# An attention and mixture-of-experts kernel whose tile loop gets fourfold key weights, summed row statistics and another order of work

## The reference

```python
def block(x, wq, bq, wk, bk, wv, bv, gamma, W1, W2, bias, expert_sel, keys, values):
    q, k, v = (einsum('bchw,oc->bohw', x, w) + b for w, b in ((wq, bq), (wk, bk), (wv, bv)))  # 32, 32, 256 channels
    energy = einsum('bci,bcj->bij', flat(q), flat(k)).reshape(b, h, w, h, w)
    attn = softmax(energy, axis=-1)                 # over rows of 32 keys
    x = gamma * einsum('bchk,bhwkv->bcwv', v, attn) + x
    t = tokens(x)                                   # (b, 1024, 256)
    u = layer_norm(t, eps=1e-5)
    # memory[n, m] = n - m where 0 < n - m <= 32, else 0
    t = t + u @ W1 + (memory @ u) @ W2 + bias
    u = layer_norm(t, eps=1e-5)
    s = sigmoid(u @ expert_sel.T)                   # 32 experts
    val, idx = top_k(s, 2)
    return t + sum over the two experts e of val_e * relu(u @ keys_e) @ values_e
```

## Time and profile before

| | |
|---|---|
| time, median of 3 runs | 505.77 us (504.06 to 508.54) |
| time of the profiled execution | 506.34 us |
| its span, first to last instruction | 504.6 us |
| PE busy | 404.9 us (80%) |
| DVE busy | 376.0 us (75%) |
| POOL busy | 323.5 us (64%) |
| ACT busy | 228.5 us (45%) |

### The profile page before, as it was taken

One profiled execution on the slowest core, in us unless ns is written; L12 is line 12 of the kernel. 1 busy time (PEld: TensorE's weight loads), 2 busy tenths in 40 slices (PEclk: granted clock), 3 DMA queues, 4 the chain that ended last, 5 costly groups with the idle time before them and its releaser, 6 DMA issues.

```text
span 504.6 us, 10093 instructions
## 1 busy us (share of the span) xinstructions
PE 404.9 (80%) x2919; PEld 307.4 (61%) x2919; DVE 376.0 (75%) x1100; ACT 228.5 (45%) x604; POOL 323.5 (64%) x481
## 2 busy tenths in 40 slices
PE   8899999999999999999999865769666597577000
PEld 4667777877778777777676753247454386466000
DVE  2788999999999999999999746648555586657100
ACT  2223554545555455545454434168555396444000
POOL 5355558888778888588888776445555645536610
PEclk9999999999999999999999887699789978878655
DMA  7996001311111111111210011386654343331096
GB/s 221 341 210 159 12 23 54 126 54 45 51 36 43 54 44 54 44 44 44 63 54 35 22 47 59 112 250 186 183 160 145 123 129 107 111 96 51 6 202 125
DMA packets 28439, 49.52 MB, mean 98 GB/s; under 512 B 6204, under 2 KB 21966, under 8 KB 27373
## 3 DMA queue, kind: packets, MB, share of 16 engines
q1 hardware_dynamic: 20512, 26.69, 20.2%
q0 software_dynamic: 7872, 22.19, 14.2%
HBM read 30.74 MB, written 25.73 MB: 112 GB/s over the span
## 4 chain that ended last, share of the span: by engine, by line
PE 48%; DVE 15%; issue 13%; SPq 12%; DMA 2%; POOL 2%; another core or an unknown queue 1%; ACT 1%; DVEq 0%; POOLq 0%; ACTq 0%
PE bank L1217 16%; SPq L412 8%; PE bank L1157 6%; PE bank L1098 5%; PE E L1122 5%; PE bank L1077 2%; PE bank L1190 2%; DVE gmax L765 2%; DVE gsum L813 2%; PE bank L1198 2%; PE bank L1269 2%; PE bank L1177 2%; SPq L274 1%; SPq L409 1%
## 5 line engine op out<-in xcount | busy, mean ns | idle before, releaser
L588 POOL DMA_INDIRECT out<-vT,dest x80 | 79.0, 988 | 63.9 <-DVE vT L1031 43.6
L1217 PE MATMUL bank<-vT,prob 128*128 128x256 f32 x512 | 118.9, 386 | 0.2 <-POOL prob L506 0.2
L1217 PEld LDWEIGHTS bank<-vT,prob 128*128 128x128 f32 x512 | 95.7, 191 | 12.7 <-POOL prob L506 0.6
L506 POOL TENSOR_TENSOR prob<-prob,ginv 128x1024 f32<-128x1024 f32 x32 | 61.1, 1909 | 27.8 <-DVE ginv L828 25.5
L488 POOL DMA_INDIRECT slot_rows<-rows,slot x64 | 68.5, 1070 | 12.6 <-issue 12.6
L685 ACT ACTIVATE prob<-E 128x512 f32<-128x512 f32 x40 | 22.4, 591 | 50.9 <-remote 21.1
L648 ACT ACTIVATE prob<-prob 128x1024 f32<-128x1024 f32 x32 | 33.8, 1056 | 20.6 <-DVE prob L769 20.6
L813 DVE TENSOR_REDUCE gsum<-prob 128x32 f32<-128x1024 f32 x32 | 38.5, 1204 | 4.1 <-ACT prob L648 4.0
L765 DVE TENSOR_REDUCE gmax<-E 128x32 f32<-128x1024 f32 x32 | 39.0, 1219 | 1.8 <-PE E L1122 1.3
L1045 DVE COPY rows<-values_s 64x256 f32 x112 | 37.5, 335 | 3.6 <-issue 2.3
L769 DVE TENSOR_TENSOR prob<-E,gmax 128x1024 f32<-128x1024 f32 x32 | 39.2, 1224 | 1.1
(11 more groups left out here) (211 smaller groups left out, 924.5 us busy)
## 6 DMA issues: line engine op xcount, KB each, us to landing
xc_or_xin<-slot_rows SPq DMA_DIRECT2D x32, 130.0 KB
xt<-x_tok SPq DMA_DIRECT2D x32, 128.0 KB, 2.3
values_s<-values SPq DMA_DIRECT2D x2, 2048.0 KB, 29.1
out<-out POOLq DMA_DIRECT2D x4, 1024.0 KB, 14.5
xc_or_xin<-x_cm SPq DMA_DIRECT2D x3, 1024.0 KB, 22.3
t<-slot_rows SPq DMA_DIRECT2D x16, 130.0 KB
t<-slot_rows SPq DMA_DIRECT2D x32, 65.0 KB
xc_or_xin<-slot_rows SPq DMA_DIRECT2D x32, 65.0 KB
```

The costliest lines, as they stand in the source:

```text
L506: g.tensor_tensor(prob[:, t % 2], prob[:, t % 2], ginv[:, t % 2].unsqueeze(2).to_broadcast([P, WT * KB, W]), ALU.mult).then_inc(prob_done, 1)
L588: g.indirect_dma_start(out=out, out_offset=bass.IndirectOffsetOnAxis(ap=dest[:, n % (2 * NB), k:k + 1], axis=0), in_=yb[:, n % NB, k, :], ...
L1217: mm = m.matmul(av_p, pr[:, j, :], vT[:, b % 2, j, :], start=(j == 0), stop=(j == KB - 1))
```

## The change

- **Fourfold k weights.** The weight tile `wqk` now holds wk four times and wq once. k comes out of TensorE in all four groups of 32 partitions and is evacuated whole; q is projected by 8 matmuls of 128 rows by 32 columns, so that the four 32-token parts of a tile land in four partition groups (`q_s[c*32:(c+1)*32]`). `energies` then uses 16 positions of the array, the row group c writing PSUM bank c of a new 4-bank tile `X`.
- **When.** q is projected in step 2 of a batch, k in quarters in steps 3 to 6. k's evacuation moves from VectorE to ScalarE (except for the first batch). v is evacuated one step later.
- **Accumulated sums.** `bn_stats` and `bn_aggr` go. The residual sums become `scalar_tensor_tensor` with `accum_out` (sum of the row), ScalarE then does `Square` of (sum - 256 x) with `accum_out`, and adds eps in another activation; GpSimd keeps the power and the shift.
- **Order on TensorE.** memory and second transpose lead, then attention, positions, logits, projections, mix, v, transpose. v waits for `t1_done` of the attention in the same step, since `v_p` shares bank 7 with `av_p`.
- **Scatters** of a tile go in one place, one step later, ahead of the second layer norm's factors on GpSimd.
- **Routing tail.** sigmoid, top-2 (`MAX`, `MAX_INDEX`) go to the end of VectorE's step, one-hot and positions' sums into the next step.

The diff, cut to its core:

```diff
-QK_STEPS = (5, 6)
+Q_STEP, K_STEPS = 2, (3, 4, 5, 6)
...
-        E = ps("E", [P, WT * KB * W])
-        bank = {i: ps(f"bank{i}", [P, 512]) for i in range(2, 8)}
+        X = ps("X", [P, 2048])
+        bank = [X[:, i * 512:(i + 1) * 512] for i in range(4)] + [ps(f"bank{i}", [P, 512])[:, :] for i in range(4, 8)]
+        E = X.rearrange("p (w c) -> p w c", w=WT)[:, :, 0:KB * W]
...
+        qk_p = bank[6][:, C:2 * C]
+        av_p = bank[7][:, 0:C]
+        v_p = bank[7][:, C:2 * C]
...
-            def layer_norm_factors(t, mv_t, mv_done, rstd, used, ve_done, rstd_done, nmr_done):
-                pool.wait_ge(mv_done, t + 1)
+            def layer_norm_factors(t, mv_t, rstd, used, ve_done, rstd_done, nmr_done):
+                pool.wait_ge(ve_done, t + 1)
                 after(pool, used, t - 1)
-                g.tensor_scalar(rstd[:, t % 2, 0:1], mv_t[:, 1:2], LN_EPS, None, ALU.add).then_inc(ve_done, 1)
...
-                for t in tiles(s, S_SEND):
-                    rows_complete(t)
-                    scatter_rows(t, 0)
+                for t in tiles(s, S_SEND + 1):
+                    send(t)
                 for t in tiles(s, S_NORM2):
                     second_factors(t)
...
+            def squared(x, mv_t, rstd_t, t, x_done, rstd_done, mv_done, ve_done):
+                act.wait_ge(x_done, t + 1)
+                after(act, ve_done, t)
+                a.activation(squares[:, :], x, ACT.Square, bias=mv_t[:, 0:1], scale=-float(C),
+                             accum_out=mv_t[:, 1:2]).then_inc(mv_done, 1)
+                act.wait_ge(mv_done, t + 1)
+                after(act, rstd_done, t - 1)
+                a.activation(rstd_t[:, 0:1], mv_t[:, 1:2], ACT.Identity, bias=eps_col[:, 0:1], scale=1.0 / C ** 3).then_inc(ve_done, 1)
...
+            def first_sum(t):
+                dve.wait_ge(av_mm, t + 1)
...
+                v.scalar_tensor_tensor(out=t1[:, t % 3], in0=av_p, scalar=1.0, in1=xt[:, t % 4], op0=ALU.mult, op1=ALU.add,
+                                       accum_out=mv1[:, t % 2, 0:1]).then_inc(t1_done, 1)
...
-                v.tensor_tensor(t2[:, t], h_at(t), t1b[:, t % 2], ALU.add).then_inc(t2_done, 1)
-                dve.wait_ge(t2_done, t + 1)
-                v.bn_stats(bn2[:, t % 2], t2[:, t]).then_inc(bn2_done, 1)
...
+            def k_proj(b, u):
+                per = HW // len(K_STEPS)
+                for a in range(CH):
+                    mm = m.matmul(qk_p, wqk[:, a, 0:4 * QK], xc[:, b % 2, a, u * per:(u + 1) * per],
+                                  start=(a == 0), stop=(a == CH - 1))
+                mm.then_inc(k_mm, 1)
+            def q_proj(b, dst):
+                for a in range(CH):
+                    tokens = xc[:, b % 2, a, :].rearrange("p (t w h) -> p w t h", w=WT, h=H)
+                    for c in range(WT):
+                        mm = m.matmul(dst[c * QK:(c + 1) * QK, :], wqk[:, a, 4 * QK:5 * QK], tokens[:, c],
+                                      start=(a == 0), stop=(a == CH - 1))
+                mm.then_inc(q_mm, 1)
...
-                for w in range(WT // 2):
+                for c in range(WT):
                     for g in range(WT):
-                        for r in range(2):
-                            at = slice((2 * r + 1) * QK, (2 * r + 2) * QK)
-                            cols = slice((r * 2 + w) * KB * W, (r * 2 + w + 1) * KB * W)
-                            mm = m.matmul(E[g * H:(g + 1) * H, cols], q_s[at, b % 2, tb, w, :],
-                                          k_s[at, b % 2, g].rearrange("p j v -> p (j v)"), start=True, stop=True)
+                        at = slice(c * QK, (c + 1) * QK)
+                        mm = m.matmul(E[g * H:(g + 1) * H, c, :], q_s[at, b % 2, tb, :],
+                                      k_s[at, b % 2, g].rearrange("p j v -> p (j v)"), start=True, stop=True)
...
+            for s in range(NT):
+                if s > 1:
+                    energies(s)
...
+                for t in tiles(s, S_NORM2):
+                    memory(t)
+                for t in tiles(s, S_ROUTE):
+                    second_turn(t)
+                for t in tiles(s, S_AV):
+                    attend(t)
+                for t in tiles(s, S_POS):
+                    positions(t)
+                for t in tiles(s, S_ROUTE):
+                    logits(t)
...
+                for t in tiles(s, S_MIX):
+                    mix(t)
+                if work:
+                    after(pe, t1_done, s)
...
+                    v_proj(work[0], work[1], v_p)
```

More of the change, by code:

```diff
@@ L641, in _ @@
[L641 to L648 removed]
+                    logits_exp(t)
                 if s == 0:
@@ L669, in _ @@
                 for t in tiles(s, S_ROUTE):
[L670 to L678 removed]
+                    columns_written(t)
@@ L824, in _ @@
-                t = tile(s, 0)
-                if t is not None:
-                    dve.wait_ge(sum_done, t + 1)
-                    after(dve, prob_done, t - 1)
-                    v.reciprocal(ginv[:, t % 2], gsum[:, t % 2]).then_inc(inv_done, 1)
+                for t in tiles(s, S_SEND):
+                    place(t)
+                for t in tiles(s, S_POS):
+                    chosen(t)
+                for t in tiles(s, S_SEND):
+                    entry_rows(t)
+                for t in tiles(s, S_POS):
+                    both_chosen(t)
@@ L1192, in _ @@
-                for t in tiles(s, S_ROUTE):
-                    pe.wait_ge(u2T_out, t + 1)
-                    after(pe, ex_done, t)
-                    if proj_work(s - 1) and proj_work(s - 1)[2]:
-                        pe.wait_ge(v_out, bank6_v[0])
-                    for a in range(CH):
-                        mm = m.matmul(lg_p, u2T[:, t % 2, a, :], sels[:, a, :], start=(a == 0), stop=(a == CH - 1))
-                    mm.then_inc(lg_mm, 1)
-                t = tile(s, S_POS)
-                if t is not None and s < NT + S_MIX:
-                    positions(t)
+                    second_turn(t)
@@ L1219, in _ @@
-                if work:
-                    for c in work[2]:
-                        qk_proj(work[0], c)
-                t = tile(s, S_TURN)
-                if t is not None:
-                    pe.wait_ge(u1_done, t + 1)
-                    after(pe, uT_lo_done, t)
-                    for a in range(CH):
-                        mm = m.transpose(uT_p[:, a, :], u1[:, t % 2, a * P:(a + 1) * P], ident[:, :])
-                    mm.then_inc(uT_mm, 1)
-                if s < NT:
-                    for t in tiles(s, S_MIX):
-                        mix(t)
-                elif s == NT + 1:
+                for t in tiles(s, S_AV):
+                    attend(t)
@@ L1234, in _ @@
+                for t in tiles(s, S_TURN):
+                    turn(t)
+                if s == NT + 1:
                     mix(NT - 1)
-                if work and work[2]:
-                    v_proj(work[0], work[1])
-                    bank6_v[0] = v_evacs[0]
             for _ in range(PLAN_WARM):
-                m.matmul(bank[7][:, :], ones_b[:, :], warm[:, :], start=True, stop=True)
+                m.matmul(bank[7], ones_b[:, :], warm[:, :], start=True, stop=True)
             pe.wait_ge(sched_done, 4)
```

634 lines of the change are left out of this document (326 added, 308 removed).

## The result

The changed kernel takes 517.08 us (median of 4 runs, 514.66 to 523.37), the kernel before 506.98 beside it. 498.5 was forecast, in a range of 493 to 507.

A forecast was written before the change was run, and what follows sets the result against it. TensorE was taken to bound the middle batches, VectorE the last. Terms -4.4 + 0.5 - 4.8 - 0.4 + 1.8 = -7.3 gave 498.5 us against the median of 505.77; range 493 to 507.

The forecast's parts named there:

- the one on the routing chain: VectorE, last batch: four dependent operations no longer interleaved cost 0.3 us more a step (0 to 0.5).
- rival (c): Slower: exponential late behind a ScalarE normalisation that waits for GpSimd, which waits for eps; 513 us, chance 0.1.
- Energies: TensorE, each step: 32 passes on 16 positions instead of 8, 0.64 us for 1.02, 0.38 saved.
- rival (a): Row groups don't overlap four deep, energies stay at 1.02 us; 506.5 us, chance 0.1.
- Two middle batches: TensorE: each full batch from 70.14 to 67.95 us through shorter energies, projections and fewer waits; -4.4 for two.
- The prediction's own ring: Energies, maximum, VectorE up to the residual sum, v, transpose, next energies; TensorE reaches v at 6.93 without a projection.
- Projections: TensorE, each batch: k stays at 3.44 us as four quarters of 0.86; q adds 1.05.
- Sums: VectorE: accumulated sums replace statistics instructions, 0.96 becomes 0.42 and 0.90 becomes 0.45, 0.99 us less a step.
- -5.2 was forecast for that batch: Last batch, VectorE-bound: seven steps of 7.5 for 8.18 us, -4.8, and the first maximum 0.4 sooner, -0.4.
- v's wait: v waits for the residual sum, ending 6.8 us after the energies' start; hidden except in the first steps.
- The head: First batch: v's unhidden wait and early k quarters delay it, steps 5 and 6 give back about 3; net +0.5.
- Drain: Behind the last maximum: longer layer norm chains and later work, against less GpSimd time; +1.8 us (-1 to +5).

The follow-up runs named there:

- a1: Changed kernel with the addition of 1 to the exponentials also writing its row sum to an unread column: 502.95 us, ratio 0.995.
- b2: Kernel of a1 with VectorE's low part of z ahead of v's evacuation: 500.93 us, ratio 0.992.
- a2: Changed kernel with the addition of 1 written as a sum of two SBUF tensors: 522.3 us, ratio 1.036.
- b1: Kernel of a1 with the statistics as before (bn_stats, bn_aggr) in place of accumulated sums and ScalarE's squares: 511.92 us.
- b4: Kernel before with the accumulated sums alone; order, energies, projections and scatters unchanged: 510.81 us, ratio 1.014.
- c1: Changed kernel, addition in its original form, GpSimd's scaling of the weights split into two instructions of half the columns: ratio 1.009.
- a3: Kernel before with one more constant addition on VectorE behind the residual sum, under GpSimd's scaling: 558.3 us, ratio 1.108.
- b3: Kernel of b2 with the one-hot comparison and its sum moved to the end of VectorE's step: 508.49 us.

## Why the prediction was wrong

The stretches of four kernels, from maximum to maximum of the tile named, in us:

| | before | forecast | after | a1 | b2 |
|---|---|---|---|---|---|
| start to tile 8 | 79.0 | 79.5 | 81.35 | 80.5 | 80.0 |
| 8 to 16 | 70.1 | 67.95 | 73.1 | 69.6 | 68.8 |
| 16 to 24 | 70.2 | 67.95 | 73.1 | 69.5 | 68.6 |
| 24 to 31 | 57.0 | 51.8 | 60.65 | 51.0 | 51.0 |
| last maximum to plan | 39.5 | 41.3 | 41.5 | 42.1 | 41.2 |
| plan to end | 188.8 | 188.8 | 191.8 | 188.8 | 188.4 |

**The step that failed** is the one on the routing chain: "no longer interleaved with other work: four dependent operations ..., 0.3 more (0 to 0.5)". I priced the moved operations by their dependences, with durations from rows in which GpSimd was elsewhere, and asked for no operation what its neighbour engine would be doing at the new place. 1.95 for 0.15 is +1.8 us of VectorE a step. It puts VectorE on the chain of six steps of eight in the middle batches and of all in the last: 9.05 for a1's 8.14 without a projection, 9.05 to 9.57 for 8.76 to 9.26 with one, and 8.65 for 7.32 in the last batch. It turned -5.6 at the last maximum (a1) into +12.0 (after): 17.6 us in the trace. By the medians a1 and after are 14 apart, a1 and a2 (held alike, on a1's chip) 19. The range's upper end of 507 contained no such term; rival (c), slower through a late exponential, had the right sign and the wrong mechanism: ScalarE and GpSimd do not stand in after's chain from tile 8 to the last maximum. Without the hold the forecast was still too good by 4 us (a1) and 2 (b2), and the terms below say where: of the -9.1 forecast at the last maximum, a1 has -5.6 and b2 -7.9.

**Energies: right in size.** 0.64 forecast, 0.64 to 0.65 measured (b2's chain), against 1.02 in the earlier trace rows: what two bursts of sixteen positions were to take, so rival (a) is out. Where VectorE waits for their end they take 0.81 for 1.11. The half that the prediction drew from the Trainium skill, TensorEngine Tiling (Array Packing), 0.51, was not reached.

**Two middle batches: -4.4 forecast, -2.9 in b2 and -1.2 in a1.** In b2 0.38 a step is gained with the energies, and memory, now right behind them, takes 0.67 for 0.47, attention 3.46 for 3.55, the second transpose 0.22 for 0.37, mix 1.47 for 1.40, the rest 0.73 for 0.63; a step is 8.04 for 8.30, where 7.93 was forecast. I carried the other pieces over from the old order unchanged. The prediction's own ring held a better number: v comes at 6.93, and with v's 0.86 and the transpose's 0.22 behind it that makes a step of 8.01. Projections: k adds 0.85 (0.86 forecast), q 1.13 (1.05). In a1 v's evacuation ahead of the low part costs another 0.1 a step.

**Sums: right.** The instructions are 0.36 and 0.42 with the read 0.08 beside them; b1 puts their worth at 0.86 us a step in the last batch (0.99 forecast). -5.2 was forecast for that batch, -6.0 came in a1 (7.3 a step for 7.5). There the bound is not VectorE, as forecast, but in most steps a ring that the prediction hadn't: TensorE's memory to mix 6.40, z's high part on ScalarE 0.39, its low part on VectorE 0.44, signals, and memory again, 7.32 us. One step in a1's chain, from the maximum at 248.83, is VectorE alone and takes 7.08. ScalarE's read of the accumulator is 0.19, of which 0.10 stands behind the square's end (0.05 forecast), and no step of b2's chain between tile 8 and the last maximum has a square in it; b4 shows such terms on the chain where the order is the old one.

**v's wait: right.** In a1 the residual sum ends 6.5 after the energies' start (6.8 forecast) and v follows the mix without a gap. Before tile 8 it binds as forecast: in after, v at 27.52 right behind the sum (27.10 + 0.36), the third energies at 28.58 (28.4 forecast, 26.75 before). The head lost 1.0 to 1.5 where 0.5 was forecast, and 2.3 in after, with the held addition.

**Drain: +1.8 forecast, +1.7 to 2.6 measured.** Behind the loop the addition isn't held, 0.17 us.

**What stays open.** By the trace a2 and after differ by 0.1 at the last maximum, and by 2.4 us in span; by medians they are 5 us apart. In after's trace the last maximum comes 12 us later than in before's and the drain is 2 us longer, which with 507 for the kernel before would make 521; the runs other than the profiled one took 514.66 to 517.66. The expert stage's length differs between executions (191.8 us in after's trace, 188.8 in before's) and was 33 us shorter on the third chip, for a reason that no run here looked for. So the hold's cost in the loop is known, 17.6, and in the whole time only as 14 to 19.

## What to carry to other kernels

Before an operation of VectorE is moved, lay GpSimd's timeline beside its new place: here a long elementwise operation there stopped small VectorE instructions that read two tensors in SBUF, or a tensor and a constant, until its end, while those with an operand in PSUM, the statistics, the reciprocal and the accumulating form passed. An instruction whose duration differed tenfold between two places at the same shape was held here, not slow; look for what ends at its end on the other engines. And a sum of terms from one order of work holds for another only if each duration is asked anew what stands beside it and ahead of it: 0.38 us gained on energies became 0.26 a step by the pieces behind them.

## What the hardware showed unasked

- A 128 x 32 addition took 0.15 to 0.18 us alone, 1.95 beside a GpSimd instruction of 1.92, 1.08 beside one of 1.05 (means of c1). The hold was always to the end of the GpSimd instruction, or 0.03 to 0.09 us past it (a3, b3).
- Held by an elementwise operation of GpSimd: tensor with constant (float32, in SBUF; 1.95 for 0.15), tensor with tensor (a2, 1.91), comparison of two tensors (b3, 0.99 for 0.22), sum of two halves of one (before's drain, 0.61 for 0.19). Not held beside the scaling: RECIPROCAL (0.35) and MAX8 (0.20) on 32 columns (a1, right behind the addition), `bn_stats` of 256 columns in SBUF (before, 0.42), subtractions with one operand in PSUM (before, 0.39 to 0.41), the accumulating addition (a1, 0.18). The Trainium skill's conditions for the 2-port modes, in VectorE: DVE Perf Modes (Mode 2×_2P), allow the first kind (float32, one source, both sides in SBUF, even sizes).
- On ScalarE, ACTIVATION_READ_ACCUMULATOR is 0.19 us and starts 0.40 behind the start of its 0.49 us square.
